# Unpadded heads in the projections of the last layer's two attention stages, and two of sixteen turned heads evicted by VectorE

## The chip, the cores and the metric

One NeuronCore of a Trainium2 chip runs the whole program in one launch. The metric is the device time in microseconds (us). TensorE is called PE, VectorE DVE, ScalarE ACT, GpSimd POOL, and SyncE, which issues the DMAs, SP.

## The reference, cut to what matters

Four transformer layers are run one after the other on `x` [8, 112, 256], with a context of [8, 375, 192]. The first three have sixteen heads of 64 columns. The fourth has sixteen heads of 16 columns, and its two attentions are what the change touches:

```python
def _decoder_block(...):                     # H = 16, HD = 16
    h = _layernorm(x, ln1_w, ln1_b)
    qkv = (h @ qkv_w + qkv_b).reshape(B, T, 3, H, HD)
    q, k, v = [qkv[:, :, i].transpose(0, 2, 1, 3) for i in range(3)]
    attn = jnp.einsum('bhtd,bhsd->bhts', q, k) * scale       # + causal and padding masks
    sa = jnp.einsum('bhts,bhsd->bhtd', jax.nn.softmax(attn, axis=-1), v)
    x = x + merge(sa) @ proj_w + proj_b
    h = _layernorm(x, ln2_w, ln2_b)
    q, k, v = heads(h @ q_w + q_b), heads(enc @ k_w + k_b), heads(enc @ v_w + v_b)
    attn = jnp.einsum('bhtd,bhsd->bhts', q, k) * scale       # + padding mask
    ca = jnp.einsum('bhts,bhsd->bhtd', jax.nn.softmax(attn, axis=-1), v)
    x = x + merge(ca) @ out_w + out_b
    ...                                                      # layer norm, GELU feed-forward
```

## The kernel before, in words

There are seven attention stages, numbered 0 to 6. Stages 0 to 4 are the wide ones; stage 5 is the fourth layer's self-attention and stage 6 its cross-attention, the two "small" stages. Each runs over the batch b = 0..7.

**Matrices.** float32 products are made of float32r parts: a weight or an activation is split into a high part and a rest (`hi`, `lo`), and a projection sums the passes hi·hi, hi·lo and lo·hi, two chunks of the 256 inputs each (six passes; five where the input is the 192-column context). One pass is one matmul.

**Padding and doubling.** Rows of TensorE are used in groups of 32 (`rows = 128 // sh.HPT`, line 1338), but a small head has 16 columns. So the kernel before pads: queries and keys are projected with every head's 16 columns twice (`twice_heads`), 512 columns in four pieces of 128; values are projected with 16 columns of zeros behind every head (`pad_heads`), 512 columns. In stage 6 the doubling carries the split: the first copy of the key rows holds the high part, the second the rest, so two passes (`query_parts`, line 1116) give the scores. In stage 5 the scores are plain float32 matmuls.

**Units of work.** `qk`, `q`, `k` and `v` are projection pieces (line 1201 issues all their matmuls); `set` is the score matmuls of four units (lines 1336 to 1384, again issued at 1201), `scores` the mask, the row maximum (DVE, lines 1718 to 1723) and the exponential (ACT, line 1572); `trans` turns one head's (stage 6) or four heads' (stage 5) probabilities on PE (line 1393) and ACT evicts them (line 1587); `av` multiplies by the values into the bank pO; `ta` (line 1438), `tb` (line 1443) and `wo` normalise, turn back and project the output; `lnt` (line 1449) turns a layer norm's rows. `ql` (DVE, line 1684) writes the queries' rest in stage 6. In the small stages POOL splits each key piece in two operations (lines 1882 and 1884) and writes the masks.

**What sets the order.** `fill(s, b, i)` gives the pieces that stand on PE behind each set, and `tensor_order()` the whole order of PE. Projection pieces, `trans`, `ta`, `tb`, `wo` and `lnt` go in turn through three PSUM banks pG0 to pG2: a piece starts when the piece three before it has been evicted (`work_start`). The scores of a unit use one of four banks pS, and a set waits until DVE has read the units four before. The other engines' orders come out of `plan()`, a list scheduler with the durations of `duration()`; on the chip each engine runs its list strictly in order. Weights come in by SP, 512 columns a time, through two buffers `wraw`; ACT writes their high part (line 1504), DVE the rest (line 1653). Four tiny DMAs (line 1157) for each small stage bring the biases of its values into `bias_c`; the biases of queries and keys come with one DMA at the start, into `bsm_sb`.

## Time and profile before

| | us |
|---|---|
| median of the runs | 1613.89 |
| lowest and highest of 3 runs | 1612.89, 1616.92 |
| span of the profiled execution, first to last instruction | 1608.7 |
| stage 5, first set to first set of stage 6 | 1291.05 to 1375.15 |
| stage 6, first set to last set | 1375.15 to 1554.85 |

The profiled execution has no time of its own beside its span; the span is 5.2 us below the median of the runs. Engines' busy times, waits and starts are counted in this one execution, in us from its first instruction. Matmuls overlap each other, so start-to-start distances tell their cost better than their durations, and a busy share of 97% of PE isn't one of PE at its peak.

### The profile page before, as it was taken

How to read it: one execution, taken by the hardware profiler on the slowest of the kernel's cores; microseconds unless marked ns; L12 is line 12 of the kernel's file. 1: busy time of each engine (PE TensorE's matmuls, PEld its weight loads, DVE VectorE, ACT ScalarE, POOL GpSimd, SP SyncE). 2: the span in 40 equal slices, each digit the busy share in tenths (PEclk: the TensorE clock that was granted, in tenths of full speed). 3: DMA queues.
4: the chain of work that ended last, by engine and by line, in shares of the span. 5: the costliest groups of instructions: out<-in, count | busy, mean ns of one | idle time of the engine just before them, and what ended most of it. 6: DMA issues, size and time to landing. Idle time of an engine off the chain costs nothing.

```text
span 1608.7 us, 38092 instructions
## 1 busy us (share of the span) xinstructions
PE 1562.6 (97%) x14070; PEld 1360.1 (85%) x14070; DVE 953.1 (59%) x2550; ACT 1037.5 (64%) x2964; POOL 845.3 (53%) x1396
## 2 busy tenths in 40 slices
PE   7999999999999999999999999999999998999998
PEld 6888788888889888878888889888888887788778
DVE  7665554545566655554545466654545678776674
ACT  6666666667643556666667652666766697678771
POOL 3665357666552644457676552457666524444421
PEclk9999999999999999999999999999999999999999
DMA  5332200001120100210001110100001110001000
GB/s 168 116 97 91 71 31 18 18 18 44 46 70 27 57 2 28 70 47 18 18 19 44 41 59 28 64 31 18 18 18 56 56 33 4 31 18 32 18 2 24
DMA packets 39558, 67.15 MB, mean 42 GB/s; under 512 B 7120, under 2 KB 14064, under 8 KB 39376
## 3 DMA queue, kind: packets, MB, share of 16 engines
q1 hardware_dynamic: 38800, 64.67, 12.4%
q8 instruction: 114, 1.87, 0.5%
q14 instruction: 68, 0.56, 0.1%
q10 hardware_dynamic: 576, 0.05, 0.0%
HBM read 59.17 MB, written 5.54 MB: 40 GB/s over the span
## 4 chain that ended last, share of the span: by engine, by line
PE 86%; ACT 5%; DVE 4%; issue 3%; POOL 1%; DMA 0%; ACTq 0%; DVEq 0%
PE pG L1201 52%; PE pG L1393 12%; PE pO L1201 12%; PE pS L1201 9%; ACT P L1574 1%; POOL P L1844 1%; PE pG L1449 1%; DVE nmax L1705 0%; DVE W L1653 0%; ACT QF_hi L1518 0%; ACT V L1560 0%; PE pG L1438 0%; DVE full L1783 0%; ACT AOT_hi L1594 0%; ACT W L1504 0%
## 5 line engine op out<-in xcount | busy, mean ns | idle before, releaser
L1844 POOL TENSOR_SCALAR P<-P,rinv 112x375 f32<-112x375 f32 (+1 forms) x640 | 326.5, 523 | 240.9 <-DVE rinv L1729 240.2
L1574 ACT ACTIVATE P<-pS,nmax 112x375 f32<-112x375 f32 (+1 forms) x640 | 308.3, 498 | 102.7 <-DVE nmax L1705 102.7
L1201 PE MATMUL pG<-hT_hi,W 128*128 128x224 f32 (+1 forms) x1408 | 317.0, 305 | 9.5 <-DVE hT_lo L1790 3.2
L1201 PEld LDWEIGHTS pG<-hT_hi,W 128*128 128x128 f32 x1408 | 238.1, 191 | 22.8 <-DVE W L1653 3.4
L1587 ACT ACTIVATE PT<-pG 125x336 f32<-125x336 f32 (+1 forms) x448 | 198.7, 469 | 87.4 <-PE pG L1393 86.9
L1201 PE MATMUL pG<-src,W 128*128 128x376 f32 (+1 forms) x1036 | 237.9, 353 | 2.3 <-DVE hid_hi_f L1667 1.1
L1393 PE MATMUL pG<-ident,P 112*125 112x112 f32 (+1 forms) x1472 | 225.9, 278 | 11.1 <-POOL P L1844 6.6
L1705 DVE TENSOR_REDUCE nmax<-pS 112x1 f32<-112x375 f32 (+1 forms) x448 | 228.2, 549 | 7.6 <-PE pS L1201 6.4
L1393 PEld LDWEIGHTS pG<-ident,P 112*125 112x125 f32 (+1 forms) x1472 | 186.1, 176 | 42.7 <-issue 9.0
L1201 PE MATMUL pG<-hT_lo,W 128*128 128x224 f32 (+1 forms) x704 | 207.6, 295 | 0.0
L1201 PEld LDWEIGHTS pG<-src,W 128*128 128x128 f32 (+1 forms) x1036 | 171.5, 188 | 30.3 <-issue 25.2
L1201 PE MATMUL pG<-W,src 128*125 128x512 f32 (+1 forms) x645 | 182.2, 404 | 0.1
L1201 PEld LDWEIGHTS pO<-PT,V 125*64 125x64 f32 (+1 forms) x2816 | 135.8, 137 | 36.7 <-issue 20.0
L1201 PE MATMUL pO<-PT,V 125*64 125x112 f32 (+1 forms) x2816 | 163.6, 264 | 1.3 <-ACT V L1560 1.0
L1729 DVE RECIPROCAL rinv<-rsum 112x1 f32<-112x1 f32 (+1 forms) x448 | 71.8, 161 | 135.4 <-ACT P L1574 130.9
L1871 POOL TENSOR_TENSOR rest<-whole_f,KF_hi 128x376 fp32r<-128x376 f32 x144 | 143.2, 995 | 12.0
L1899 POOL TENSOR_TENSOR rstd<-ve,mhalf 112x1 f32<-112x1 f32 x80 | 50.0, 625 | 176.9 <-DVE ve L1639 176.6
L1574 ACT ACTIVATION_READ_ACCUMULATOR P<-pS,nmax 112x1 f32 x640 | 139.7, 218 | 0.0
L1201 PEld LDWEIGHTS pG<-hT_lo,W 128*128 128x128 f32 x704 | 134.2, 191 | 3.1
L1201 PEld LDWEIGHTS pG<-W,src 128*125 128x125 f32 (+1 forms) x645 | 113.7, 186 | 21.0 <-DVE AOT_lo L1756 0.3
L1201 PE MATMUL pG<-W,AOT_hi 128*112 128x256 f32 x704 | 129.2, 284 | 1.8 <-DVE AOT_lo L1740 1.4
L1869 POOL TENSOR_SCALAR KF_hi<-whole_f 128x376 fp32r<-128x376 f32 x144 | 74.4, 516 | 90.0 <-DVE whole_f L1672 81.0
(139 smaller groups left out, 3009.6 us busy)
## 6 DMA issues: line engine op xcount, KB each, us to landing
wraw<-wts SPq DMA_DIRECT2D x110, 256.0 KB, 2.6
src<-ctx_split SPq DMA_DIRECT2D x64, 282.0 KB, 3.0
ctx_split<-hid_lo_t SPq DMA_DIRECT2D x8, 564.0 KB, 3.6
whole_f<-wts SPq DMA_DIRECT2D x14, 256.0 KB, 6.0
V<-ctxT SPq DMA_DIRECT2D x8, 376.0 KB, 4.2
src_half<-ctx_split SPq DMA_DIRECT2D x21, 94.0 KB, 3.1
bo_b<-bo SPq DMA_DIRECT2D x10, 112.0 KB, 3.3
out<-x SPq DMA_DIRECT2D x8, 112.0 KB, 1.9
```

The lines of the kernel that those rows point to most:

```text
L1201: return nc.tensor.matmul(o, l, r, start=first, stop=last)
L1393: ins = nc.tensor.transpose(g[0:sh.krows, i * T:(i + 1) * T], lhsT, ident[0:T, 0:T])
L1449: ins = nc.tensor.transpose(g[:, k * T:(k + 1) * T], hn[:, n % 2, k * 128:(k + 1) * 128], ident[0:T, 0:T])
L1574: ins = act.activation(o, pS[U % 4][0:T, i * n:(i + 1) * n], ACT.Exp, bias=nmax[:, r, i:i + 1], accum_out=rsum[:, r, i:i + 1])
L1587: act.activation(o[0:sh.krows, 0:n], g[0:sh.krows, 0:n], ACT.Copy).then_inc(pt_ready, 1)
L1705: dve.tensor_reduce(nmax[:, r, 0:sh.G], ps, AX.X, ALU.max, negate=True).then_inc(maxed, 1)
L1729: dve.reciprocal(rinv[:, r, 0:sh.G], rsum[:, r, 0:sh.G]).then_inc(recip, 1)
L1844: ins = pool.tensor_scalar(o, o, rinv[:, r, i:i + 1], st.nscale, ALU.mult, ALU.mult)
L1869: pool.tensor_scalar(KF_hi[:, t, :], keys_rest(t, whole_f), 1.0, 1.0, ALU.mult, ALU.mult).then_inc(k_part, 1)
L1871: pool.tensor_tensor(keys_rest(t), keys_rest(t, whole_f), KF_hi[:, t, :].bitcast(F32), ALU.subtract).then_inc(k_split, 1)
L1899: pool.tensor_tensor(rstd[:, r:r + 1], ve[:, r:r + 1], mhalf[:, :], ALU.pow).then_inc(ln_rstd, 1)
```

## The change

- Queries and keys of stages 5 and 6 are projected without doubling, 256 columns in two pieces of 128; values without padding, 256 columns. `half_empty` names the weight chunks of which only every other 16 columns are now converted, so ACT and DVE convert 256 columns of these chunks and not 512. The DMAs of the weights are the same.
- Two heads now share 32 rows. The even head's scores use its 16 rows alone (`head_rows`). For the odd head POOL writes a copy of the queries in which the even head's rows are zero (`qm`, new line 1953, one for each query piece); its scores use all 32 rows.
- In stage 6 the keys' two parts now lie in two tiles, so a head's scores take three passes instead of two. POOL still does two operations for a key piece, but there are two pieces a batch instead of four.
- The biases of queries and keys come through the tiny DMAs too: twelve for each small stage instead of four.
- Of the sixteen turned heads of a batch in stage 6, DVE evicts numbers 5 and 13 (`turned_by_dve`).
- In stage 6 the first set of a batch stands before the `av` on PE again, and `wo` moves from behind the third set to behind the fourth.

```diff
 ...
+def half_empty(item, c):
+    return item in (26, 29) or item in (27, 28) and c < 2
...
+    def small_head(self, i, r):
+        p = i % 2 ^ r // 2
+        return 8 * (i // 2) + 2 * r + p
...
+def turned_by_dve(e):
+    return e.kind == "trans" and e.s == 6 and e.i % 8 == 5
...
         if pr < NPAIR - 1:
-            out += [Ev("qk", s, pr + 1, 2 * odd + j) for j in range(2)]
+            out.append(Ev("qk", s, pr + 1, odd))
...
     if not last:
-        keys = ((0, 1), (2,), (3,), ()) if b else ((), (0,), (1,), (2, 3))
+        keys = ((0,), (1,), (), ()) if b else ((), (0,), (1,), ())
...
-        if pr < NPAIR - 1 and i in (0, 2):
-            out.append(Ev("q", s, pr + 1, 2 * odd + i // 2))
+        if pr < NPAIR - 1 and i == 0:
+            out.append(Ev("q", s, pr + 1, odd))
...
-        if d.s == 5 and d.b < 3 or d.s == 6 and d.i == 0 and d.b:
+        if d.s == 5 and d.b < 3:
             order += [held.pop(0), d]
...
-                    for t in range(2):
-                        for k in range(2):
-                            four = bsm[:, 3 * s - 13, t + 2 * k:t + 2 * k + 1].rearrange("(r j) c -> r j c", r=4)
...
+                    for i in range(3 * s - 15, 3 * s - 12):
+                        for t in range(2):
+                            for k in range(2):
+                                four = bsm[:, i, t + 2 * k:t + 2 * k + 1].rearrange("(r j) c -> r j c", r=4)
...
+        def head_rows(sh, h):
+            t, r = sh.score_place(h)
+            rows = 128 // sh.HPT
+            return slice(rows * r, rows * r + (16 if sh.HPT == 4 and t % 2 == 0 else rows))
...
+                    cols = 256 if st.small else 512
...
-                        for p in range(2 if s == 6 else 0):
+                        for p in range(3 if s == 6 else 0):
                             for u in us:
...
+                                ins = mm(pS[u % 4][0:T, 0:SP], query_part(b, t, p == 2)[rg],
+                                         hid_hi_t[rg, k_tile(s, b, t // 2 * 2 + (p == 1)), 0:SP], p == 0, p == 2)
...
+                elif e.kind == "trans":
+                    U = unit(e)
+                    dve.wait_ge(transposed, U + 1)
+                    o, n = turned(U)
+                    wait(dve, attended, n)
+                    dve.tensor_copy(o[0:KM, 0:3 * T], g_bank(e)[0:KM, 0:3 * T]).then_inc(ptd_ready, 1)
...
+                    pool.tensor_scalar(o, whole, lo_rows_sb[:, 0:1], 1.0, ALU.mult, ALU.mult).then_inc(qm_ready, 1)
```

Before the last batch of stage 4 no engine's order changes but for sizes and one small POOL operation (`bq`), which moves from the start to behind the biases. From there on the lists differ.

PE, stage 6, in the middle of a batch, before. pS is a set, pO an `av`, `ident,KF` turned heads (three matmuls each), `src,W` a key piece, `ident,PT` (L1443) a `tb`, `hT_hi,W` and `hT_lo,W` a query piece:

```order
L1201 MATMUL pS<-hid_hi_t,hid_lo_t 112x376 x8
L1201 MATMUL pO<-QF,V 32x112 x12
L1393 MATMUL pG<-ident,KF 125x112 x3
L1201 MATMUL pG<-src,W 128x376 x5
L1393 MATMUL pG<-ident,KF 125x112 x3
L1443 MATMUL pG<-ident,PT 128x112 x2
L1393 MATMUL pG<-ident,KF 125x112 x3
L1201 MATMUL pG<-hT_hi,W 128x224
L1201 MATMUL pG<-hT_lo,W 128x224
L1201 MATMUL pG<-hT_hi,W 128x224 x2
```

The same place after, where `W,src` is a value piece:

```order
L1248 MATMUL pS<-hid_hi_t,hid_lo_t 112x376 x12
L1248 MATMUL pO<-QF,V 32x112 x12
L1445 MATMUL pG<-ident,KF 125x112 x6
L1248 MATMUL pG<-W,src 125x256 x5
L1445 MATMUL pG<-ident,KF 125x112 x6
L1500 MATMUL pG<-ident,PT 128x112 x2
```

The set has a third pass, the key and the query piece are gone from this place, and between the turned heads stands one value piece of 256 columns.

PE, stage 5, between `ta` (L1438) and the values of a batch, before; `ident,hid_lo_f` are turned heads and `W,hT_hi` and `W,hT_lo` the value piece:

```order
L1438 MATMUL pG<-ident,PT 112x128 x4
L1393 MATMUL pG<-ident,hid_lo_f 112x112 x4
L1201 MATMUL pG<-hT_hi,W 128x224
L1201 MATMUL pG<-hT_lo,W 128x224
...
L1201 MATMUL pG<-W,hT_hi 112x512 x2
L1201 MATMUL pG<-W,hT_lo 112x512
```

And after:

```order
L1495 MATMUL pG<-ident,PT 112x128 x4
L1445 MATMUL pG<-ident,hid_lo_f 112x112 x4
L1248 MATMUL pG<-W,hT_hi 112x256 x2
L1248 MATMUL pG<-W,hT_lo 112x256
L1248 MATMUL pG<-W,hT_hi 112x256 x2
```

One of the batch's two query-and-key pieces (twelve matmuls of 224 columns) is gone from between them, and the value piece is half as wide.

SP, in stage 1 near its end, where the biases of stage 6 are loaded between weights, before:

```order
L1151 DMA wraw<-wts 128x512 x4
L1167 DMA src<-ctx_split 128x564 x2
L1151 DMA wraw<-wts 128x512
L1157 DMA bias_c<-bsm 64x1x1 x4
L1151 DMA wraw<-wts 128x512 x3
```

And after:

```order
L1197 DMA wraw<-wts 128x512 x4
L1214 DMA src<-ctx_split 128x564 x2
L1197 DMA wraw<-wts 128x512
L1204 DMA bias_c<-bsm 64x1x1 x12
L1197 DMA wraw<-wts 128x512 x3
```

Eight more DMAs stand ahead of three weight loads, and the lists of ACT and DVE, which convert those weights in order, are the same there as before.

## Rows read from the trace of the kernel before

**Rows 1.** The page: busy time of the engines; the chain, by engine.

```profile
PE 1562.6 (97%) x14070; PEld 1360.1 (85%) x14070; DVE 953.1 (59%) x2550; ACT 1037.5 (64%) x2964; POOL 845.3 (53%) x1396
...
PE 86%; ACT 5%; DVE 4%; issue 3%; POOL 1%; DMA 0%; ACTq 0%; DVEq 0%
```

**Rows 2.** Stretches: us, busy PE, PEld, DVE, ACT, POOL, PEclk, DMA share, GB/s.

```profile
1274.40:1283.15 8.75, 8.75 (x86) 7.96 (x85) 4.82 (x13) 5.55 (x15) 2.36 (x4) 1.00 0.26 86
...
1299.08:1306.28 7.20, 6.78 (x104) 5.95 (x105) 5.80 (x10) 7.20 (x24) 1.88 (x7) 1.00 0.02 4
...
1327.38:1337.84 10.46, 9.99 (x124) 8.45 (x124) 8.30 (x20) 9.23 (x31) 3.65 (x8) 1.00 0.01 3
...
1361.53:1375.15 13.62, 12.37 (x134) 10.48 (x133) 10.21 (x24) 9.27 (x29) 5.78 (x10) 1.00 0.01 2
1375.15:1405.50 30.35, 27.41 (x312) 22.65 (x312) 23.02 (x75) 19.23 (x45) 14.21 (x22) 1.00 0.08 23
...
1449.19:1471.33 22.14, 21.68 (x241) 17.84 (x237) 15.31 (x50) 17.20 (x40) 9.61 (x14) 1.00 0.10 30
...
1515.67:1536.69 21.02, 20.36 (x229) 16.43 (x225) 14.62 (x48) 16.34 (x38) 9.27 (x14) 1.00 0.01 2
```

**Rows 3.** Timeline of stage 6: start, us, engine, line, operation, idle before.

```profile
1450.37 0.82 PEld L1201 LDWEIGHTS pG<-src,W 128*128 128x128 f32 x5
...
1451.17 0.47 PEld L1393 LDWEIGHTS pG<-ident,KF 112*125 112x125 f32 x3
...
1453.62 0.28 PEld L1201 LDWEIGHTS pS<-hid_hi_t,hid_lo_t 32*112 32x112 f32 x8
...
1454.15 0.54 PEld L1201 LDWEIGHTS pO<-QF,V 125*32 125x32 f32 x24 [0.25 <-issue]
...
1457.34 0.99 PEld L1201 LDWEIGHTS pG<-W,src 128*125 128x125 f32 x5
...
1458.38 0.53 PEld L1393 LDWEIGHTS pG<-ident,KF 112*125 112x125 f32 x3
```

**Rows 4.** The chain that ended last, one query piece in stage 6.

```profile
1453.02 0.68 PE pG L1201 x6
```

**Rows 5.** Timeline of stage 5: `wo` and `ta`; values and `trans`; a `qk` piece and `trans`.

```profile
1320.89 0.47 PE L1201 MATMUL pG<-W,AOT_hi 128*112 128x256 f32 x2
...
1321.80 0.65 PE L1438 MATMUL pG<-ident,PT 128*112 128x128 f32 x4
...
1324.03 0.68 PE L1201 MATMUL pG<-W,hT_hi 128*112 128x512 f32 x2
...
1325.47 0.55 PE L1393 MATMUL pG<-ident,P 112*112 112x112 f32 x4
...
1329.63 0.35 PE L1201 MATMUL pG<-hT_hi,W 128*128 128x224 f32 x1
...
1331.05 0.55 PE L1393 MATMUL pG<-ident,hid_lo_f 112*112 112x112 f32 x4
```

**Rows 6.** Groups in 1405.5 to 1515.67: busy us, mean ns, idle before by releaser.

```profile
L1587 ACT ACTIVATE QF<-pG 125x336 f32<-125x336 f32 x80 | 34.1, 449 | 17.3 <-PE pG L1393 17.0
L1393 PEld LDWEIGHTS pG<-ident,KF 112*125 112x125 f32 x240 | 32.4, 187 | 9.8 <-DVE hid_hi_f L1667 3.6 <-issue 2.8 <-DVE AOT_lo L1756 1.3
...
L1667 DVE TENSOR_SCALAR hid_hi_f<-pG,bsm_sb 128x376 f32<-128x376 f32 x20 | 12.1, 607 | 1.2 <-PE pG L1201 1.2
...
L1737 DVE COPY PT<-pO 128x448 f32<-128x448 f32 x5 | 3.1, 614 | 0.0
```

**Rows 7.** Timeline of stage 1: the bias DMAs, the loads behind them, a conversion.

```profile
417.53 2.35 SPq L1157 DMA_DIRECT2D bias_c<-bsm  x4
...
419.92 5.66 SPq L1151 DMA_DIRECT2D wraw<-wts  x3
...
423.23 0.66 ACT L1504 ACTIVATE W<-wraw 128x512 fp32r<-128x512 f32 x1
```

**Rows 8.** The page: DMA issues; KB each, us from issue to landing.

```profile
wraw<-wts SPq DMA_DIRECT2D x110, 256.0 KB, 2.6
```

More of the change, by code:

```diff
@@ L90, in __init__, with score_place @@
         self.per = self.NS // self.NO
+    def small_head(self, i, r):
+        p = i % 2 ^ r // 2
+        return 8 * (i // 2) + 2 * r + p
+    def score_place(self, h):
+        if self.HPT == 2:
+            return h // 2, h % 2
+        return 2 * (h // 8) + h % 2, h // 2 % 4
     def heads(self, u):
+        if self.HPT == 2:
+            return [2 * (4 * (u // 2) + j) + u % 2 for j in range(4)] if self.G > 1 else [u]
         if self.G == 1:
[L95 to L98 removed]
+            return [self.small_head(u // 4, u % 4)]
+        return [self.small_head(i, u) for i in range(4)]
     def units(self, i):
@@ L108, in tiles @@
     def tiles(self, us):
-        return sorted({t for u in us for t, _ in self.heads(u)})
+        return sorted({h // (8 if self.HPT == 4 else 2) for u in us for h in self.heads(u)})
 STAGES = make_stages()
@@ L280, in fill @@
         if last and s == 4:
-            out += [Ev("qk", 5, 0, t) for t in ((0,), (1, 2), (3,), ())[i]]
+            out += [Ev("qk", 5, 0, t) for t in ((0,), (1,), (), ())[i]]
         if i == 2:
@@ L327, in fill @@
         out.insert(1, Ev("tb", s, b - 1))
+    if b and i == (2 if last else 3):
         out.append(Ev("wo", s, b - 1))
@@ L439, in duration @@
     if engine == "sp":
-        return .06
+        return .7 if k == "bias" else .06
     if engine == "pe":
         if k == "set":
-            return 1.25 if st.self_ else .7 if st.small else 1.2 if split(e.s, e.b) else 1.75
+            return 1.25 if st.self_ else .65 if st.small else 1.2 if split(e.s, e.b) else 1.75
         if k == "trans":
@@ L832, in program @@
         assert [(e.i, e.m) for e in order[engine] if e.kind == "w"] == [(c, n) for n, (_, c) in enumerate(CHUNKS)]
-    for engine, kind in (("act", "scores"), ("dve", "scores"), ("pool", "norm"), ("act", "trans")):
+    for engine, kind in (("act", "scores"), ("dve", "scores"), ("pool", "norm")):
         units = [unit_no(e.s, e.b, e.i) for e in order[engine] if e.kind == kind]
         assert units == list(range(BASE[5] if kind == "norm" else BASE[6] + B * H))
+    turns = [unit_no(e.s, e.b, e.i) for e in order["act"] if e.kind == "trans"]
+    assert turns == [U for U in range(BASE[6] + B * H) if not turned_by_dve(Ev("trans", *UNITS[U]))]
     with ExitStack() as ctx:
@@ L978, in columns, with chunk @@
             a = CHUNKS[n][1] * WQ
-            return slice(a, a + (C if packed(n) else WQ))
+            return slice(a, a + (C if packed(n) or half_empty(*CHUNKS[n]) else WQ))
+        def chunk(n, hl):
+            o, view = W[:, SLOT_OF[CHUNKS[n][0]], hl, columns(n)], raw(n)[1]
+            if half_empty(*CHUNKS[n]):
+                return o.rearrange("p (h d) -> p h d", d=16), heads_of(view, 0)
+            return o, view[:, 0:columns(n).stop - columns(n).start]
         def res_of(e):
@@ L1063, in hid_free @@
             else:
-                wait(eng, scored, scored_after(6, B - 1, 2 * (t - 4) + 1) if t > 3 else scored_after(6, B - 2, 7))
+                wait(eng, scored, scored_after(6, B - 1, 2 * ((t - 4) | 1) + 1) if t > 3 else scored_after(6, B - 2, 7))
         def half_free(eng, s):
@@ L1337, in _ @@
                     else:
-                        accumulate(g[0:sh.krows, :], passes).then_inc(pieces, 1)
+                        accumulate(g[0:sh.krows, 0:cols], passes).then_inc(pieces, 1)
                 elif e.kind == "set":
@@ L1342, in _ @@
                     n = T if st.self_ else SP
-                    rows = 128 // sh.HPT
                     for us in sh.beside(e.i):
                         for t in sh.tiles(us):
+                            if st.small:
+                                wait(pe, qm_ready, qm_no[Ev("qm", s, b // 2, t)])
                             if s == 5 and b > 1:
@@ L1411, in _ @@
                     for us in sh.beside(e.i):
-                        wait(pe, pt_ready, unit(e, us[-1]) + 1)
+                        for u in us:
+                            f = Ev("trans", s, b, u)
+                            if f in ptd_no:
+                                wait(pe, ptd_ready, ptd_no[f])
+                            else:
+                                wait(pe, pt_ready, pt_no[f])
                         for i in range(sh.G):
@@ L1502, in _ @@
                         wait(act, pieces, item_last[before[-1]])
-                    cols = columns(n)
-                    act.activation(W[:, SLOT_OF[item], 0, cols], view[:, 0:cols.stop - cols.start], ACT.Copy).then_inc(w_hi, 1)
+                    o, view = chunk(n, 0)
+                    act.activation(o, view, ACT.Copy).then_inc(w_hi, 1)
                 elif e.kind == "q":
@@ L1511, in _ @@
                             wait(act, transposed, BASE[6] if b else 0)
-                        act.activation(hid_lo_t[:, q_tile(s, 2 * b, e.i), 0:PAIR], g[:, 0:PAIR], ACT.Identity,
-                                       bias=bsm_sb[:, 3, e.i:e.i + 1]).then_inc(q_ready, 1)
+                        wait(act, bias_in, 384)
+                        act.activation(hid_lo_t[:, q_tile(s, 2 * b, 2 * e.i), 0:PAIR], g[:, 0:PAIR], ACT.Identity,
+                                       bias=bias_c[:, 3, e.i:e.i + 1]).then_inc(q_ready, 1)
                     else:
```

151 lines of the change are left out of this document (81 added, 70 removed).

## The prediction

> **What bounds the kernel now.** I read the page first. PE is busy 97% of the span and holds 86% of the chain that ended last, while no other engine passes 64% [rows 1]. So a matmul taken out counts, as long as nothing else is late in its place. Whether that holds has to be read by stage, since the change lies in the last 320 us alone. The second view is busy time from set to set [rows 2]. In the steady part of stage 6 a batch takes 22.14 us, with PE busy 21.68, ACT 17.20, DVE 15.31 and POOL 9.61. In stage 5 a batch takes 10.46 us, with PE 9.99, ACT 9.23 and DVE 8.30. PE bounds both, but DVE and ACT stand close behind in stage 5, and at 1299 to 1306 ACT is busy 7.20 of 7.20 us. The granted clock is 1.00 (2.4 GHz) in all these rows. The third view is the timeline, for the start-to-start price of each piece.
>
> **Prices of what goes.** A key piece holds PE from 1450.37 to 1451.17, 0.80 us [rows 3]. A query piece in stage 6 costs 0.68 [rows 4]. A query-and-key piece in stage 5 runs from 1329.63 to 1331.05, 1.42 us [rows 5]. For the values the rows give a price per matmul. The six of 512 columns run from 1324.03 to 1325.47, 0.24 each; the six of 256 columns of a `wo`, from 1320.89 to 1321.80, 0.15 each [rows 5]. So each narrowed matmul saves 0.09, which is 0.54 for six in stage 5 and 0.45 for five in stage 6. The five of 512 there take 1.04 (1457.34 to 1458.38 [rows 3]), 0.21 each.
>
> Removed from PE: stage 5's 16 qk pieces become 8, 8 x 1.42 = 11.4; 8 value pieces x 0.54 = 4.3; stage 6's 32 key pieces become 16, 16 x 0.80 = 12.8; 16 query pieces become 8, 8 x 0.68 = 5.4; 24 value pieces x 0.45 = 10.8. Sum 44.7 us.
>
> **Price of what is added on PE.** Each of the 32 sets of stage 6 gets a third pass of four matmuls that lie beside each other in four row groups. Two passes now take 0.53 (1453.62 to 1454.15 [rows 3]), at most 0.27 each. A matmul of the same 376 columns costs 0.80 / 5 = 0.16 in a key piece, the lower bound. I take 0.17, near the lower end, since the eight weight loads of a set take only 0.28 together and so don't pace it. 32 x 0.17 = 5.4 us, with 8.6 at the upper bound. Net off PE: 39.3 us. Half-filled row groups (16 of 32 rows) occur nowhere in this trace; see the second rival.
>
> The Trainium skill would price the values otherwise: in "TensorE: Matmul & The Clock Gate", section "Back-to-back issue gap", it gives about 81 ns for a matmul of 128 columns in a real kernel and 131 for one of 512. Drawn straight between them, 256 columns would cost some 98, a narrowed matmul would save 0.033 us and the 168 of them 5.5 us instead of 15.1, so the forecast would lie near 1593. The trace, with 0.21 to 0.24 at 512 columns, disagrees, and I stay with it.
>
> **The other engines in stage 6, per batch.** ACT loses two of sixteen evictions (2 x 0.45 [rows 6]) and one query eviction, about the same each: 17.20 goes to some 15.9. DVE loses two key evictions (2 x 0.61 [rows 6]) and one query rest, and gains two copies of 336 columns. Such a copy doesn't stand in the trace; ACT's 0.45 for the same tile is the lower bound and DVE's 0.61 for 448 columns the upper [rows 6], and I take 0.50. DVE goes to about 14.7. POOL loses two of four key splits and gains one `qm`; at 9.61 of 22.14 us it has room, also for the mask loads that it waits for in order. So in stage 6 the order of limits stays: PE near 19.2, ACT 15.9, DVE 14.7. In stage 5 ACT loses one pair of evictions and falls below 8.5, PE falls to 10.46 - 1.42 - 0.54 = 8.5, and DVE stays at 8.30. There DVE's row of masks and maxima becomes as late as PE. A `qm` for stage 5 is due a batch after its piece is made, and POOL is busy 3.65 of 10.46 us, so I cost it at nothing; if POOL had no room, each would cost what it takes, under 1 us for the 16.
>
> **Where cover is lost.** A piece waits for the eviction of the piece three before. Now two turned heads stand between a key piece and the next piece with one more piece around them; after, the pieces between are shorter (0.59 instead of 1.04 for the values) or are turned heads, which are shorter still. PE's weight loads for turned heads already wait 9.8 us in five batches, 3.6 of it for DVE's key evictions [rows 6]. I add 0.45 us a batch in stage 6 and take 0.7 off each batch's gain in stage 5 for DVE.
>
> **The biases.** Four tiny DMAs hold SP 2.35 us, 0.59 each [rows 7]. Twelve hold it 8 x 0.59 = 4.7 us longer. Behind them stand three weight loads. The first is issued at 419.92 and its conversion on ACT starts at 423.23 [rows 7], 3.3 us later. After the change it is issued at 424.6, and with 2.6 us to landing [rows 8] ACT would stand from 423.2 to about 427.3. ACT is in order: exponentials and evictions queue behind, and DVE behind its own half of the conversion. PE has work ahead for about one set, so between 0 and 4.1 us arrive on it; I take 3.0, since PE bounds there and doesn't get it back. The other twelve stand ahead of context loads for a later batch, with no conversion waiting for SP: nothing. The narrower conversions save ACT and DVE some 0.3 us each in stage 4, where PE is busy 8.75 of 8.75 us [rows 2]: nothing.
>
> **The sum.** By stretch, net removal first and what I take of it behind. Last batch of stage 4: two qk pieces and a value piece, 3.4, taken 3.2 (PE 8.75 of 8.75). First two batches of stage 5: 3.4, taken 2.2 (ACT full, relieved by the same pieces). The next four: 7.8, taken 5.2. The last two, which also hold the first keys and queries of stage 6: 2 x 0.80 + 2 x 0.68 + 2 x 0.54 + 2 x 0.45 = 4.9, taken 4.0 (PE busy 12.37 of 13.62). Stage 6, batch 0 (30.35 us): 1.6 + 0.7 + 1.8 - 0.7 = 3.4, taken 3.0. Batches 1 to 5: 1.6 + 0.68 + 1.35 - 0.68 = 2.95 each, taken 2.5, so 12.5. Batch 6 (21.02 us, no queries): 2.3, taken 2.1. Batch 7 has nothing to remove and four longer sets: -0.7. Together 31.5 us, less 3.0 for the biases, 28.5 us. The profiled span of 1608.7 would become 1580.2. The median lay 5.2 above its span, and I keep that distance: 1613.9 - 28.5 = **1585.4**. The tail behind 1558 is the same work.
>
> **The rivals.**
> *Banks and readers take over.* The Trainium skill says so in "TensorEngine Tiling (Array Packing)", section "PSUM Bottleneck": faster matmuls leave the eviction as the bound; the trace of before, bound by PE, doesn't show it yet. As a mechanism here: an eviction by ACT (0.45) often stands behind an exponential, and with only 0.7 to 0.9 us between a piece and the third after it, PE waits at most pieces; in stage 5 DVE's 8.30 plus its latencies hold the batch at 10.0. Steady batches of stage 6 at 20.6 give 7.5 instead of 12.5; with batch 0 at 2.0, batch 6 at 1.5, stage 5 at 1.5 + 2.0 + 2.5, the last batch of stage 4 at 3.0, less 0.7 and 4.1 for the biases, the gain is 15.2: 1598.7. For it speaks ACT's full 7.20; against it that PE in stage 5 reaches 9.99 of 10.46 beside an ACT at 88% and a DVE at 79%, closer than stage 6 will be.
> *Half-filled row groups don't run beside full ones*: slower. If the matmuls of a set ran one after the other, stage 6's twelve would take 12 x 0.16 = 1.92 instead of 0.70, 32 x 1.2 = 39 us more. Stage 5's eight sets have 32 passes each; at the 1.42 / 12 = 0.12 of a pass of a qk piece that is at most 3.8 us a set, 30 in all, and I take half: 1585.4 + 39 + 15 = about 1639. It decides as soon as a set costs 28.5 / 40 = 0.7 us more than I price. Against it: full row groups do overlap (eight matmuls in 0.53 us where a row would need 1.28), and weight tiles of 112 and 125 rows cost no more than those of 128.
> *All of it arrives*: DVE keeps ahead in stage 5, the `av` behind the set removes the waits for key evictions, and the bias DMAs are hidden: 39.3 off gives 1574.6.
> *The gain is eaten up* by the two together, a stall at the biases and sets at the upper bound with waits beyond the first rival: about 1611.
>
> **Chances.** Forecast, 1577 to 1594: 0.64. First rival, 1594 to 1604: 0.20. All of it, below 1577: 0.06. Eaten up, within 0.3% (1609 to 1618.7): 0.04; between 1604 and 1609: 0.02. Slower: 0.04. The range reaches over forecast and first rival, 1576 to 1603, and leaves out under 0.2. About 0.3% is what a measurement of this kernel can tell from no change. Faster 0.92, same 0.04, slower 0.04.
>
> **What would show it.** Right: steady batches of stage 6 at 19.2 to 20.0 us from set to set; of stage 5 near 9.3; PE still busy over 95% there; a set, start to the `av` behind it, near 0.70; value pieces of stage 6 near 0.6; a wait of ACT of 3 to 4 us at about 423 us, and everything from there to stage 4 some 3 us later. Wrong: stage 6 above 20.5 with waits of PE for ACT's or DVE's evictions (first rival), sets above 1.4 us (second), or no wait at the biases and stage 4 starting as before, which would strike my 3.0.

## The result and the profile after

The changed kernel takes 1587.53 us (median of 4 runs, 1587.27 to 1590.88) beside 1613.76 for the kernel before: a ratio of 0.9837, 95% interval 0.9822 to 0.9851, 26.2 us less. The prediction was 1585.4 in a range from 1576 to 1603, so it was right, 2.1 us too low. The profiled execution spans 1585.9 us, 22.8 less than that of before.

The page of after: busy time of the engines; the chain by engine [rows 1 show before].

```profile
PE 1525.5 (96%) x13974; PEld 1332.3 (84%) x13974; DVE 945.0 (60%) x2538; ACT 1021.7 (64%) x2928; POOL 825.8 (52%) x1380
...
PE 83%; DVE 7%; ACT 4%; issue 3%; POOL 1%; DMA 1%; SPq 1%; DVEq 0%; ACTq 0%; POOLq 0%
```

PE's busy time fell by 37.1 us, near the 39.3 of the sum, but DVE's share of the chain grew from 4% to 7%: some of the removed work left waits behind. Where, the stretches from set to set show (us, busy PE, PEld, DVE, ACT, POOL, PEclk, DMA share, GB/s). The first four are batches 2 to 5 of stage 5, then batch 0, two steady ones and batch 6 of stage 6, and 14 us of the tail:

```profile
1308.69:1317.60 8.91, 8.66 (x97) 7.96 (x97) 7.15 (x16) 8.91 (x30) 1.60 (x4) 1.00 0.01 2
1317.60:1329.06 11.46, 7.67 (x113) 6.78 (x113) 10.77 (x27) 10.24 (x32) 4.18 (x8) 1.00 0.21 61
1329.06:1339.06 10.00, 9.18 (x113) 8.16 (x113) 7.99 (x17) 7.31 (x24) 2.00 (x4) 0.83 0.01 3
1339.06:1347.83 8.77, 8.05 (x114) 6.76 (x113) 8.26 (x20) 7.88 (x27) 3.50 (x7) 1.00 0.03 7
...
1368.31:1395.73 27.42, 23.18 (x287) 19.32 (x287) 21.45 (x72) 17.74 (x44) 12.80 (x21) 1.00 0.09 25
...
1433.64:1452.67 19.03, 18.27 (x238) 15.34 (x237) 14.77 (x49) 16.08 (x37) 6.94 (x11) 1.00 0.12 34
1452.67:1472.01 19.34, 18.27 (x238) 15.35 (x238) 15.08 (x49) 16.09 (x37) 6.94 (x11) 1.00 0.12 34
...
1491.06:1510.32 19.26, 17.73 (x232) 14.61 (x231) 14.32 (x48) 15.69 (x36) 6.34 (x10) 1.00 0.01 2
...
1538.00:1552.00 14.00, 10.48 (x76) 8.91 (x68) 6.85 (x13) 4.92 (x9) 5.24 (x6) 0.52 0.00 1
```

Beside [rows 2], stage 6 is as forecast: 19.0 to 19.3 us a steady batch instead of 22.14, with PE busy 18.27 of them, ACT 16.1, DVE 14.8. Stage 5 is not. In its batch 3, PE is busy for only 7.67 of 11.46 us while DVE is busy for 10.77, and in the batch behind it the granted clock falls to a mean of 0.83; before, it was 1.00 in all of stage 5. Batch 3 is even 1.0 us longer than before, where DVE was already busy for 9.71 of its 10.48 us; [rows 2] have the lighter batch 4. The stretch of batch 3 in the kernel before:

```profile
1316.90:1327.38 10.48, 9.72 (x125) 8.45 (x125) 9.71 (x22) 10.22 (x32) 2.15 (x3) 1.00 0.18 52
```

The timeline of after (start, us, engine, line, operation, idle before and what ended it) shows the longest waits ahead of sets, two in stage 5 and one in stage 6:

```profile
1301.38 1.05 PE L1248 MATMUL pS<-KF,QF 16*112 16x112 f32 x32 [1.41 <-DVE nmax L1776]
...
1329.06 1.05 PE L1248 MATMUL pS<-KF,QF 16*112 16x112 f32 x32 [3.19 <-DVE nmax L1776]
...
1385.03 0.77 PE L1248 MATMUL pS<-hid_hi_t,hid_lo_t 16*112 16x376 f32 x12 [1.36 <-DVE nmax L1779]
```

A set writes all four score banks, so it waits until DVE has taken the maxima of the set before. The wait in stage 6 isn't new. The kernel before has it ahead of the same set, and there the clock stayed at 1.00:

```profile
1391.05 0.60 PE L1201 MATMUL pS<-hid_hi_t,hid_lo_t 32*112 32x376 f32 x8 [1.36 <-DVE nmax L1723]
```

Batches 1 to 5 of stage 6 as one stretch, before and then after:

```profile
1405.50:1515.67 110.17, 108.08 (x1188) 89.03 (x1185) 75.93 (x248) 84.61 (x193) 48.55 (x72) 1.00 0.10 30
```

```profile
1395.73:1491.06 95.33, 91.04 (x1184) 76.57 (x1184) 72.52 (x240) 80.17 (x180) 33.44 (x53) 1.00 0.12 35
```

PE's busy time fell by 17.0 us and its idle time rose from 2.1 to 4.3. So more work went than the 14.75 us of the sum, and new waits took 2.2 us back. Both show in the timeline of PE. Before, a key piece (five matmuls) and a value piece, each with what follows it:

```profile
1450.40 1.11 PE L1201 MATMUL pG<-src,W 128*128 128x376 f32 x5
1451.34 0.48 PE L1393 MATMUL pG<-ident,KF 112*125 112x112 f32 x3
...
1457.37 1.40 PE L1201 MATMUL pG<-W,src 128*125 128x512 f32 x5
1458.61 0.48 PE L1393 MATMUL pG<-ident,KF 112*125 112x112 f32 x3
```

After, a query piece that waits for DVE's key eviction, and a value piece:

```profile
1457.06 0.37 PE L1248 MATMUL pG<-hT_hi,W 128*128 128x224 f32 x1 [0.54 <-DVE hid_hi_f L1723]
...
1462.16 0.84 PE L1248 MATMUL pG<-W,src 128*125 128x256 f32 x5
1462.84 0.48 PE L1445 MATMUL pG<-ident,KF 112*125 112x112 f32 x3
```

From the start of one to the start of the next, a key piece takes 0.94 us, and a value piece 1.24 before and 0.68 after. Against the forecast, by stretch in us (a minus is a loss):

| Stretch | forecast | measured |
|---|---|---|
| Start-up, before the biases | 0 | -2.0 |
| The biases | -3.0 | -3.3 |
| Last batch of stage 4 | 3.2 | 2.8 |
| Stage 5, batches 0 and 1 | 2.2 | 0.1 |
| Stage 5, batches 2 to 5 | 5.2 | 3.0 |
| Stage 5, batches 6 and 7 | 4.0 | 6.3 |
| Stage 6, batch 0 | 3.0 | 2.9 |
| Stage 6, batches 1 to 5 | 12.5 | 14.8 |
| Stage 6, batches 6 and 7 | 1.4 | 0.7 |
| From the last set to the end | 0 | -2.5 |
| Sum | 28.5 | 22.8 |

The 2.0 us of the start-up were already lost at the first set of the program, at 20.86 us instead of 18.90. The thirteen profiles of kernels with the change have that set at 19.23 to 22.75 us, so most of this row is scatter.

### The profile page after: what moved, and what is told of

It reads as the page before. It is cut to its first block, busy times and chain, and to the rows that moved or that the text cites. A ratio compares the mean times of both kernels' runs of the same rounds, so it can differ in the third digit from the quotient of the medians.

```text
span 1585.9 us, 37814 instructions
## 1 busy us (share of the span) xinstructions
PE 1525.5 (96%) x13974; PEld 1332.3 (84%) x13974; DVE 945.0 (60%) x2538; ACT 1021.7 (64%) x2928; POOL 825.8 (52%) x1380
## 4 chain that ended last, share of the span: by engine, by line
PE 83%; DVE 7%; ACT 4%; issue 3%; POOL 1%; DMA 1%; SPq 1%; DVEq 0%; ACTq 0%; POOLq 0%
PE pG L1248 49%; PE pO L1248 12%; PE pG L1445 12%; PE pS L1248 9%; ACT P L1631 1%; DVE KF L1779 1%; PE pG L1506 1%; DVE nmax L1761 0%; DVE bn L1691 0%; DVE nmax L1776 0%; DVE W L1709 0%; ACT W L1560 0%; ACT QF_hi L1575 0%; SPq L1204 0%; DVE hid_hi_f L1723 0%
## 5 line engine op out<-in xcount | busy, mean ns | idle before, releaser
L1248 PE MATMUL pG<-hT_hi,W 128*128 128x224 f32 (+1 forms) x1312 | 300.5, 308 | 9.7 <-DVE hT_lo L1852 3.4
L1248 PEld LDWEIGHTS pG<-hT_hi,W 128*128 128x128 f32 x1312 | 225.1, 193 | 22.5 <-DVE W L1709 3.6
L1248 PE MATMUL pG<-src,W 128*128 128x376 f32 (+1 forms) x956 | 220.2, 353 | 0.5 <-ACT whole_f L1579 0.2
L1248 PE MATMUL pG<-hT_lo,W 128*128 128x224 f32 (+1 forms) x656 | 196.2, 299 | 0.0
L1248 PEld LDWEIGHTS pG<-src,W 128*128 128x128 f32 (+1 forms) x956 | 158.4, 188 | 28.1 <-issue 25.3
L1248 PE MATMUL pG<-W,src 128*125 128x512 f32 (+2 forms) x645 | 168.6, 383 | 3.2 <-DVE hid_lo_f L1859 1.4
L1248 PEld LDWEIGHTS pO<-PT,V 125*64 125x64 f32 (+1 forms) x2816 | 135.9, 137 | 36.2 <-issue 19.3
L1248 PEld LDWEIGHTS pG<-hT_lo,W 128*128 128x128 f32 x656 | 126.7, 193 | 3.1
L1248 PEld LDWEIGHTS pG<-W,src 128*125 128x125 f32 (+1 forms) x645 | 108.9, 186 | 21.3 <-DVE hid_lo_f L1859 1.5
```

The costliest lines, as they stand in the source:

```text
L1248: return nc.tensor.matmul(o, l, r, start=first, stop=last)
```

## Experiments

Each is an edit of the changed kernel. In five comparisons the kernel before gave 1612.5 to 1613.8 us. Since single runs of one kernel scatter by 2 to 7 us, I read each effect from its stretch, and take the medians for the sum. While the clock agrees, two profiles of one order agree within a few hundredths of a us for a batch of stage 5, and within 0.35 us for one of stage 6.

### The changed kernel again

No edit.

> The changed kernel itself once more, beside the three edits of it that run with it, so that edits worth 1 to 4 us are compared on one chip. Every theory expects its earlier 1587.5 us within 1 us, 26.2 us less than the kernel before.

1590.11 us (1588.31 to 1592.43), ratio 0.9853 (0.9840 to 0.9867). The span is 2.7 us longer than in the first profile, and nearly all of it, 2.47 us, lies in stage 6's batch 0 (29.89 us instead of 27.42). The same wait of 1.36 us stands ahead of the same set, but here the set lasts 1.27 us instead of 0.77. Timeline, then a stretch of this run:

```profile
1384.83 1.27 PE L1248 MATMUL pS<-hid_hi_t,hid_lo_t 16*112 16x376 f32 x12 [1.36 <-DVE nmax L1779]
```

```profile
1384.00:1392.00 8.00, 7.17 (x56) 6.34 (x57) 4.34 (x15) 3.87 (x9) 2.51 (x4) 0.57 0.00 0
```

The same stretch of the first profile:

```profile
1384.00:1392.00 8.00, 6.68 (x80) 5.53 (x80) 5.70 (x19) 5.27 (x12) 3.27 (x5) 1.00 0.01 2
```

Behind that wait PE was given half its clock (1.2 GHz) in one execution and not in the other, and did 56 matmuls in 8 us instead of 80. That is part of the scatter between runs. It is also part of what the change cost: the mean clock of the kernel before is 0.993 to 0.997 in its runs, that of the changed kernel 0.988 to 0.992, and in the profile of before the clock stayed at 1.00 from stage 5 to the tail. Why it fell behind this wait, which was there before the change too, isn't shown.

### The biases of stage 6 loaded early

```
-        task("sp", Ev("bias", s), not_before=250. + 200. * (s - 5))
+        task("sp", Ev("bias", s), not_before=250. + 30. * (s - 5))
```

> The twelve bias DMAs of stage 6 are issued some 150 us earlier, at about 264 us, where SP waits for a context load; nothing else moves. Theory (the three weight loads behind them at 419.5 us come 4.7 us late and TensorE ends up 3.3 us behind, for good): the sets of stage 4 start 3.3 us earlier, the time falls by 3.3 us to 1584.2, and the wait of ScalarE for a raw weight at about 425 us is gone. Rival (the 3.3 us between the two profiles are chance, such as the clock granted in the first 60 us, or are given back later): no change, 1587.5 within 0.7.

1587.02 us (1586.63 to 1588.75), 3.1 less than the changed kernel beside it; ratio 0.9836 (0.9822 to 0.9849). The four weight loads go out in a row, and the conversion that came at 429.71 comes at 424.33. Timeline of after, then of this run:

```profile
419.52 6.96 SPq L1204 DMA_DIRECT2D bias_c<-bsm  x12
426.52 4.90 SPq L1197 DMA_DIRECT2D wraw<-wts  x3
...
429.71 0.63 ACT L1560 ACTIVATE W<-wraw 128x512 fp32r<-128x512 f32 x1 [4.36 <-DMA wraw<-wts]
```

```profile
263.60 7.05 SPq L1204 DMA_DIRECT2D bias_c<-bsm  x12
...
418.25 8.43 SPq L1197 DMA_DIRECT2D wraw<-wts  x4
```

The first set of stage 5 starts at 1289.32 instead of 1293.60; 0.9 of these 4.3 us were there before the biases, 3.4 are theirs. The theory holds: twelve DMAs of 64 four-byte elements stalled the conversions behind them, and PE never got it back. The tail was 1.2 us longer here, again at half clock. So the medians don't show it by themselves: the intervals of the two kernels still touch, and the changed kernel's first ratio, 0.9837, is the same as this one's.

### The last batch's turned heads by ScalarE, then all of them

```
-    return e.kind == "trans" and e.s == 6 and e.i % 8 == 5
+    return e.kind == "trans" and e.s == 6 and e.i % 8 == 5 and e.b < B - 1
```

> VectorE evicts its two turned heads of sixteen in seven batches of stage 6, and in the last batch ScalarE evicts all. Theory (the 2.5 us that the tail got longer come from the last batch's order, where ScalarE loads its gelu table before the last turned head is evicted and VectorE's copy stands behind 1.43 us of hidden-layer work): from the last set to the end 53.9 us again instead of 56.3, the time falls by 2.0 us (1.5 to 2.5) to 1585.5. Rival (the longer tail is the granted clock of 0.50 that lasts 12 us there instead of 9, whoever evicts): no change, 1587.5 within 0.7, and the clock stays at 0.50 for the 12 us.

and, in the next kernel,

```
-    return e.kind == "trans" and e.s == 6 and e.i % 8 == 5
+    return False
```

> ScalarE evicts all sixteen turned heads in every batch of stage 6. Theory (ScalarE, 15.9 us of work in a batch of 19.1, takes 0.9 back and still has room, so these evictions are worth little in the steady part): steady batches 19.1 to 19.6 us; with the tail 2.0 us shorter the time is 1585.5 to 1588. Rival (with pieces and turned heads this close together the eviction is the bound, and VectorE's part is what let all of the removed matmul time arrive): steady batches at 20.0 us or more, 1590 to 1593.

The first: 1588.59 us (1584.87 to 1589.35), ratio 0.9839. Its tail is 51.75 us instead of 56.33, more than expected, with the clock at 1.00 nearly throughout; half-clock stretches elsewhere (batch 6 of stage 6 took 20.79 us) ate part of it. The second: 1585.32 us (1583.82 to 1588.56), ratio 0.9824 (0.9811 to 0.9838), 4.8 under the changed kernel beside it but only 2.2 under that kernel's first median, and tail 54.88. Timelines of the end of the last batch, of after and of the first of these two:

```profile
1540.12 0.45 ACT L1644 ACTIVATE QF<-pG 125x336 f32<-125x336 f32 x1 [0.81 <-PE pG L1445]
1540.45 0.49 DVE L1786 COPY QF<-pG 125x336 f32<-125x336 f32 x1
1540.59 1.28 ACT L1668 ACT_TABLE_LOAD   x1
...
1541.89 0.95 ACT L1668 ACTIVATE hid_lo_f<-hid_lo_f 128x896 f32<-128x896 f32 x1
...
1542.74 0.43 ACT L1644 ACTIVATE QF<-pG 125x336 f32<-125x336 f32 x1
...
1543.32 1.35 PE L1248 MATMUL pO<-QF,V 125*32 125x112 f32 x24 [1.69 <-ACT QF L1644]
...
1545.40 1.10 PE L1495 MATMUL pG<-ident,PT 128*112 128x128 f32 x4 [0.74 <-DVE PT L1799]
```

```profile
1544.81 1.57 ACT L1644 ACTIVATE QF<-pG 125x336 f32<-125x336 f32 x4
1546.39 1.28 ACT L1668 ACT_TABLE_LOAD   x1
...
1546.52 0.78 PE L1248 MATMUL pO<-QF,V 125*32 125x112 f32 x24 [0.44 <-ACT QF L1644]
...
1548.04 0.65 PE L1495 MATMUL pG<-ident,PT 128*112 128x128 f32 x4 [0.74 <-DVE PT L1799]
```

With a copy on DVE the plan puts ACT's table load and a gelu, 2.2 us, ahead of the last turned head, for which the last `av` and all behind it wait. PE waits 1.69 us ahead of this `av`; where ACT evicts all, 0.44. The second profile of the changed kernel (*The changed kernel again*) tells the order from the clock, since it has full clock up to this `av`:

```profile
1545.41 1.35 PE L1248 MATMUL pO<-QF,V 125*32 125x112 f32 x24 [1.26 <-ACT QF L1644]
```

It starts 13.11 us after the last set, and in the kernel with the edit, also at full clock, 10.97: the order alone costs 2.1 us. The rest goes with the clock. The nine profiles with that order have tails of 56.3 to 57.8 us, the four where ACT evicts all of the last batch 51.75, 53.30, 54.74 and 54.88, and the mean granted clock of the tail is 0.88 in after and 0.99 in the kernel with 51.75 us. In the kernel before it is 0.90 with a tail of 53.85, though ACT evicts all there. So the theory holds for most of the 2.5 us, and the rival's clock is a second cost, which the old order had too.

In the steady part the eviction by DVE is worth nothing: steady batches take 19.1 to 19.4 us without it, and batches 1 to 7 together 133.5 instead of 133.8.

### Wide values again

```
-                    cols = 256 if st.small else 512
+                    cols = 512
```

> The changed kernel with the 168 matmuls of the small stages' value pieces 512 columns wide again; conversions and evictions stay narrow. Prices by the rows of before: 0.09 us for a matmul, 0.45 for a value piece of stage 6, 0.54 for one of stage 5. Theory (stage 6 is bound by TensorE; in the first six batches of stage 5 it waits for VectorE and ScalarE, and these waits also bring its clock down, so the wider matmuls are hidden there): steady batches of stage 6 grow from 19.1 to 20.5 us, stage 5 by less than 2 us in all, and the time is 11 to 13 us above the changed kernel's 1587.5 to 1590: about 1600. Rival (TensorE bounds both stages): 15.1 more, 1603. Second rival (a narrowed matmul saves 0.033 us, as drawn between the skill's two prices): 5.5 more, 1594, and steady batches at 19.6.

1598.91 us (1597.53 to 1600.43), ratio 0.9910 (0.9895 to 0.9925): 10.1 us above the mean of the changed kernel's two medians (1588.8), a little under the theory's 11 to 13. Batches 1 to 6 of stage 6 take 122.26 us instead of 114.59, so the 90 widened matmuls cost 7.67 us, 0.085 each, against the 0.09 of the sum. PE's busy time there grew by more, from 108.77 to 117.61 us, 0.098 each: 1.2 us of the wider matmuls went into idle time. In stage 5, batches 3, 5 and 6 take 11.47, 8.77 and 10.14 us, as in the narrow kernel to 0.01 us: there the narrow values bought nothing. Stage 5 as a whole grew by 3.0 us (77.69 instead of 74.71), more than the theory's 2: 1.9 in its last batch, which also holds two value pieces of stage 6, and 1.4 in batch 4, at half clock for longer. The stretch of batch 3:

```profile
1318.21:1329.68 11.47, 8.24 (x114) 7.07 (x113) 10.50 (x26) 10.50 (x32) 4.19 (x8) 0.99 0.21 61
```

PE is 0.57 us busier and waits 2.62 instead of 3.19. This is what tells a stage that is bound by PE from one that is not. The second rival, 0.033 us a matmul, falls.

### Two passes instead of three

```
-                        for p in range(3 if s == 6 else 0):
+                        for p in range(2 if s == 6 else 0):
```

(the last pass is then p == 1, and closes the sum)

> The third pass of stage 6's sets is left out, so the low part of the queries is missing from the scores. Theory (it costs 0.17 us a set, as the duration of 0.77 for twelve matmuls against 0.60 for eight shows, all of it on the path): sets of 0.60 us, steady batches at 18.4 us instead of 19.1, 5.4 us less in all. Rival (0.27 us a set, half of a set of two passes): 8.6 us less. Second rival (stage 6 without it falls under what VectorE and ScalarE need, 15 to 16 us and their latencies): less than 3 us off and new waits at the sets.

1588.40 us (1585.74 to 1590.45): no gain to be measured. A set falls from 0.77 to 0.60 us, as priced. Timeline of this run, then of after:

```profile
1442.99 0.60 PE L1248 MATMUL pS<-hid_hi_t,hid_lo_t 16*112 16x376 f32 x8
1443.52 0.78 PE L1248 MATMUL pO<-QF,V 125*32 125x112 f32 x24
```

```profile
1452.67 0.78 PE L1248 MATMUL pS<-hid_hi_t,hid_lo_t 16*112 16x376 f32 x12
1453.38 0.78 PE L1248 MATMUL pO<-QF,V 125*32 125x112 f32 x24
```

But from the first set of batch 1 to the last set, over 27 sets, it brings 3.1 us, 0.12 each of the 0.17. In batches 1 to 5 PE's idle time is 4.8 us instead of 4.3, so a little of the saving became waiting, though no new wait stands at the sets. Then stage 6's batch 0 (28.45) and the tail (57.76) are longer at half clock, 2.5 us together. The mean clock of its timed runs is 0.986 to 0.990, the lowest of all. The theory's price of a set is right, but not that all of it arrives; the time is within the second rival's 3 us, without its waits. Whether the edit lowered the clock isn't shown: two kernels with the full sets have batches 0 of 29.9 us, and two have tails of 57.5 and 57.8.

### Even heads with all 32 rows

```
-            return slice(rows * r, rows * r + (16 if sh.HPT == 4 and t % 2 == 0 else rows))
+            return slice(rows * r, rows * r + rows)
```

> Heads that use 16 of their 32 rows in the sets of stages 5 and 6 use all 32, so those heads' scores also hold the neighbour's product. Theory (half-filled row groups cost what full ones do): sets stay at 1.05 us in stage 5 and 0.77 in stage 6, the time within 0.7 us of the changed kernel apart from what the granted clock scatters. Rival (rows count, a half-filled group streams or loads faster): sets longer by up to a quarter, 0.2 us each in 40 sets, 8 us more.

1588.27 us (1586.04 to 1590.57). The sets stay at 1.05 and 0.77 us (`32*112` where after has `16*112`), and every batch of stage 6 agrees with after within 0.35 us. A half-filled row group costs what a full one does, as the prediction took it.

```profile
1446.98 0.78 PE L1248 MATMUL pS<-hid_hi_t,hid_lo_t 32*112 32x376 f32 x12
```

### The last conversions later

```
-                    w_turn = max(w_turn + W_GAP, ready_at[user])
+                    w_turn = max(w_turn + (9. if user[1].m > 123 else W_GAP), ready_at[user])
```

> The last four weight chunks are converted 9 us apart instead of 3, so VectorE and ScalarE do one conversion less in each of the batches 2 to 4 of stage 5 and more in its last batches and stage 6. Theory (in stage 5 VectorE is the bound: it is busy 10.77 of 11.46 us from 1317.6 to 1329.1 with three conversions, and TensorE's wait of 3.19 us there ends with it and is followed by a clock of 0.50): that batch takes 10.0 us or less, the wait falls under 1.5 us, the clock stays at 1.00, and stage 5 is 1.5 to 3 us shorter: 1585 to 1586 at the same clock elsewhere. Rival (what VectorE gives back is needed by the masks, ScalarE or POOL next): the waits move, less than 0.7 us.

1589.90 us (1587.97 to 1590.88): nothing gained. Batch 3 of stage 5 falls from 11.46 to 10.36 us, but batch 4 takes 12.01 with 7 us of half clock and batch 5 9.75 instead of 8.77. The wait ahead of the fifth set is 1.22 us, as the theory had it under 1.5, with DVE busy for 9.07 us in batch 3 instead of 10.77. But the clock falls behind it all the same. So these conversions made most of that wait; what falls is the theory that stage 5 gets shorter without it (75.43 us instead of 74.71).

### A shorter maximum in stage 5

```
-dve.tensor_reduce(nmax[:, r, 0:4], po, AX.X, ALU.max, negate=True).then_inc(maxed, 1)
+dve.tensor_reduce(nmax[:, r, 0:4], po[:, :, 0:T // 4], AX.X, ALU.max, negate=True).then_inc(maxed, 1)
```

> In stage 5 the row maximum that VectorE takes for the exponentials is taken over the first quarter of the columns of each head (28 of 112); any reference value serves there as long as nothing overflows. The reduce falls from 0.62 to about 0.25 us, four in a batch, 1.5 us less on VectorE in every batch of stage 5. Theory (VectorE is what kept stage 5's gain from arriving): the waits of TensorE for the maxima (1.41 us ahead of the second set, 3.19 ahead of the fifth) shrink by about as much, the clock stays at 1.00 there, batches 2 to 5 take 35 to 37 us instead of 39.1 and stage 5 is 3 to 6 us shorter than its 74.7 to 75.6. Rival (ScalarE, busy 7 to 10 us of each batch, sets the pace): less than 1 us shorter.

1585.03 us (1583.02 to 1585.81), ratio 0.9824 (0.9811 to 0.9837). Stage 5 takes 72.51 us instead of 74.71, between theory and rival. The waits shrink from 1.41 to 0.36 and from 3.19 to 2.49 us, and half clock still follows the latter. But the gain didn't come where the theory had it. Batches 2 to 5 take 39.4 us, not 35 to 37 (39.1 in after), since batch 4 is longer at half clock; 1.1 us came in batch 0 and 1.5 in batches 6 and 7. The stretch of batch 3:

```profile
1314.29:1325.06 10.77, 7.67 (x114) 6.79 (x113) 9.38 (x27) 10.48 (x33) 4.17 (x8) 0.99 0.22 65
```

With 1.4 us taken from DVE the batch shortens by 0.7, and ACT is busy for 10.48 of 10.77 us. DVE and ACT are both near full in this batch, each a link of the chain from set to set; relieving one shows the other.

### Filling the wait

```
+                    if (s, b, e.i) in FILL:
+                        wait(pe, ao_out, mask_no(s, b - 2 * (s == 5)))
+                        for _ in range(FILL[s, b, e.i]):
+                            nc.tensor.transpose(pO[:, 448:512], ident[0:64, :], ident[0:64, 0:64])
```

with `FILL = {(5, 4, 0): 24, (6, 0, 2): 10}`, at the head of a set.

> TensorE turns a constant into an unused corner of a PSUM bank 24 times ahead of the fifth set of stage 5, where it waits 3.19 us for VectorE, and 10 times ahead of the third set of stage 6, where it waits 1.36 us; nobody reads the result. Theory (the granted clock of 0.50 that follows these waits comes from the idle time, and costs 1.2 to 2.5 us each time): the clock stays at 1.00 from 1320 to 1400 us, the fifth batch of stage 5 takes 9.5 us instead of 10.0 to 11.5, stage 6's first batch 27.4 instead of up to 29.9, and the time falls by 2 to 4 us. Rival (the clock falls by chance or from the lighter work ahead of the wait): both dips stay, no change. Second rival (the turns take longer than the wait): the sets start later and the time grows by up to 2 us.

1587.69 us (1583.25 to 1590.44). At stage 6's set the idle time fell to 0.60 us, the clock stayed at 1.00 and batch 0 took 27.41 us; but four other kernels had that without filling, so one profile doesn't settle it. At the fifth set of stage 5 the 24 turns took 1.72 us, 1.53 stayed idle, and the clock fell:

```profile
1327.46 1.72 PE L1394 MATMUL pO<-ident 64*128 64x64 f32 x24
...
1330.72 1.85 PE L1249 MATMUL pS<-KF,QF 16*112 16x112 f32 x32 [1.53 <-DVE nmax L1781]
```

Neither theory nor rival was decided; half a filling was too little. This profile also has half clock at the first set of stage 5 (batch 0 takes 9.41 us instead of 7.78), so its total doesn't tell either.

### Both edits, and both with the wait filled

Early biases and `return False`, as above:

> The changed kernel with the biases of stage 6 loaded early and all turned heads evicted by ScalarE, the two edits that each shortened a stretch alone. Theory (they add up: 3.3 us at the biases, 0.3 to 0.8 in the last two batches of stage 6 and 1.5 to 4.6 in the tail): 1582 to 1584, 4 to 6 us under the changed kernel run beside such edits (1587.5 to 1590). Rival (what the earlier start gives is lost to a lower clock later, as the single run with early biases had a tail of 57.5 us): 1586 or more.

1583.21 us (1580.35 to 1583.69), ratio 0.9808 (0.9795 to 0.9822). They add up, although stage 5 has two half-clock stretches in this profile (76.92 us). And with `FILL = {(5, 4, 0): 42, (6, 0, 2): 14}` beside them:

> The kernel with early biases and all turned heads evicted by ScalarE, with filling turns again: 42 ahead of the fifth set of stage 5 (3.0 us of the 3.19 us wait, where 24 left 1.53 us idle and the clock still fell) and 14 ahead of the third set of stage 6 (1.16 us). Theory (the clock falls behind idle time, and filling nearly all of the wait keeps it up): the fifth batch of stage 5 takes 9.5 to 10.0 us instead of 11.2, stage 6's first batch 27.4 to 28 instead of 29.3, the clock shows 1.00 at both places, and the time falls from 1583.2 to about 1580. Rival (the turns, or the light work ahead of the wait, don't keep the clock up): both dips stay, 1583.2 within 1.5.

1579.66 us (1578.12 to 1580.68), ratio 0.9794 (0.9778 to 0.9811). It has the lowest median, 32.8 us under the kernel before and, by ratio, faster than the changed kernel (0.9837 and 0.9853). From the same kernel without turns it isn't told apart by the ratios, whose intervals overlap; that comparison rests on the stretches of one profile each and on the clocks of the runs. Timeline of this run, then its stretch of batch 4 of stage 5:

```profile
1321.08 2.86 PE L1394 MATMUL pO<-ident 64*128 64x64 f32 x42
1324.33 1.05 PE L1249 MATMUL pS<-KF,QF 16*112 16x112 f32 x32 [0.39 <-DVE nmax L1781]
...
1377.52 1.09 PE L1394 MATMUL pO<-ident 64*128 64x64 f32 x14
1378.95 0.77 PE L1249 MATMUL pS<-hid_hi_t,hid_lo_t 16*112 16x376 f32 x12 [0.34 <-DVE nmax L1784]
```

```profile
1324.33:1332.92 8.59, 8.00 (x112) 6.74 (x112) 7.52 (x17) 7.18 (x24) 2.00 (x4) 1.00 0.02 3
```

Batch 3 still takes 11.46 us, so the turns delay nothing. The batch behind it takes 8.59 instead of 10.00 to 11.5, since its work runs at full clock, and the clock shows 1.00 through all of stages 5 and 6 up to the tail. This set was followed by half clock in all twelve other profiles of kernels with the change. Of the changed kernel's eight timed runs the mean clock is 0.988 to 0.992; of this one's five 0.994 to 0.997, the kernel before's level. The theory holds at this set; at stage 6's, where five kernels kept their clock without turns in their profiles, the run only agrees with it.

## Why the prediction was right, point by point

- **PE bounds, so a removed matmul counts.** Right in stage 6: PE is busy 91.04 of 95.33 us in batches 1 to 5, and wide values cost 0.085 of the 0.09 us each. That 14.8 us arrived, as much as the net removal of 14.75, is an accident of two terms. The step *Where cover is lost* took 0.45 us a batch off for waits, and its size was right: idle time rose by 2.2 us in the five batches, 0.44 each. Its place was right only in part: PE's waits for DVE's key evictions grew from 1.7 to 2.3 us, and 1.9 us of new waits stand at the sets, for the maxima. What failed is *Prices of what goes*. I had read the key and value pieces of stage 6 from the weight loads (PEld), which run beside the matmuls and don't show their full price. By PE's own starts a key piece costs 0.94 us and not 0.80, and a narrowed value piece saves 0.56 (0.49 by the busy time of the kernel with wide values) and not 0.45. So PE's busy time fell by 17.0 us, and 12.5 was 2.3 too low.
- **Other prices.** From the start of a set of twelve matmuls to the `av` behind it pass 0.71 us against 0.53 for eight, so 0.18 for the third pass where 0.17 was taken; DVE's copy takes 0.50 (0.45 to 0.61 had been the bounds); a half-filled row group costs what a full one does. The 1593 that the prediction gives for a saving of 0.033 us a matmul counts only four fifths of the difference of 9.6 us; in full it would have been 1595.
- **Stage 5.** The terms *taken 2.2* and *taken 5.2* for batches 0 to 5 were mis-sized: 3.1 arrived instead of 7.4. I had named DVE as the next to be late and taken 0.7 a batch off, but with its 8.30 us of one batch, and I had taken the removed pieces off the batch's 10.46 us and not off PE's busy 9.99. In the batch before that one DVE was busy for 9.71 of 10.48 us and ACT for 10.22, before the change. Nor had I followed the chain: the set waits for the maxima of the one before, and narrower pieces ahead of that wait only make it longer. After, DVE is busy for 10.77 of 11.46 us in batch 3 beside an ACT at 10.24. The last two batches gave 6.3 instead of 4.0. There PE's busy time fell by 5.7 us, more than the 4.9 of the sum, and its idle time by 0.5; which pieces make the difference wasn't taken apart.
- **The clock.** No step had it. Waits of 1.2 to 3.2 us ahead of a set were followed by 1.2 GHz, not each time. By the rows of the first profile this cost 1.4 us in batch 4 of stage 5 (10.00 against 8.59 at full clock) and 0.6 in batch 1 (7.31 against the 6.70 of other runs), and up to 2.5 in batch 0 of stage 6 where it came.
- **The biases.** 3.0 was taken, 3.3 and 3.4 were measured, on the path for good.
- **The tail.** *The same work* was right, and the 0 wrong: the order around the DVE copy in the last batch puts a table load ahead of an eviction, which by itself costs 2.1 us, and the tail grew by 2.5 us. I had looked at that copy only as a price in steady batches; the order of its queue in the last batch was there to be read.
- **The rivals.** *Banks and readers take over* was the mechanism of stage 5. In stage 6 it is there only in the 0.44 us a batch, and its 7.5 us for batches 1 to 5 was half of what came. Slow half-filled row groups are excluded. The errors partly cancelled: +4.6 us in stage 5's last two batches and stage 6's steady ones, -10.3 in the other rows of the table; and the distance from span to median was 1.6 us instead of the 5.2 assumed. That is luck: the sum over the stretches was 5.7 us too high.

## What to carry to other kernels

When an engine at 97% gets lighter, go through each place where it now waits. What is saved there is idle time, and behind the longest of these waits TensorE ran at half clock in all twelve profiles in which the wait wasn't nearly filled, so a saving may bring nothing. Read prices from TensorE's own starts and not from those of its weight loads, and read every batch of a stage, not one. Widening one kind of matmul again tells per batch where the engine still bounds; where it doesn't, leave the work or fill the wait. And when an operation moves to another engine, look at its last instance too, where the queue around it holds other things, and at what stands behind small DMAs on the issuing queue.
